# Two transformer layers on one core: quantised probabilities clipped in SBUF and turned by a transposing DMA instead of TensorE, with a new table for the order planner

## What is computed

```
def _fq(x, delta, zp, n_bits):
    xi = _round_ste(x / delta) + zp
    xq = jnp.clip(xi, 0.0, 2.0 ** n_bits - 1.0)
    return (xq - zp) * delta
...
sim = jnp.einsum('bhid,bhjd->bhij', _fq(q, dq, 128.0, 8), _fq(k, dk, 128.0, 8)) * SCALE
attn = jax.nn.softmax(sim, axis=-1)
out = jnp.einsum('bhij,bhjd->bhid', _fq(attn, dw, 0.0, 8), _fq(v, dv, 128.0, 8))
```

## Time and profile before

| | |
|---|---|
| three runs | 3339.07, 3340.45, 3344.31 us, median 3340.45 |
| span of the profiled execution | 3338.1 us (the page gives only its span) |
| the two parts in it | transformer to about 2740 us, experts the rest, 598 us |
| busy over the span | PE 2950.0 us, DVE 2154.6, ACT 1961.0, POOL 1582.2 |

### The profile page before, as it was taken

How to read it: one execution, slowest core, us unless ns; L and a number is a source line. 1 busy time by engine, 2 the same in 40 slices (tenths; PEclk the granted TensorE clock), 3 DMA queues, 4 the chain that set the end, 5 groups by cost and what they waited for, 6 DMA issues and landing times. The chain is left out here.

```text
span 3338.1 us, 59016 instructions
## 1 busy us (share of the span) xinstructions
PE 2950.0 (88%) x19138; PEld 1701.6 (51%) x19138; DVE 2154.6 (65%) x4580; ACT 1961.0 (59%) x4178; POOL 1582.2 (47%) x2774
## 2 busy tenths in 40 slices
PE   6888998999998998989999889988988859999992
PEld 3445443544454354435443544454435229999991
DVE  4887796888678777967896788778556511111115
ACT  3666667576758676676767576757354404444442
POOL 4665472575367355726663575456434321111115
PEclk9999899999999999999999999998988879999996
DMA  3003221422142214313230412141433239999995
GB/s 95 17 23 67 60 65 29 89 61 54 32 86 60 56 37 88 77 29 72 64 69 26 89 45 57 32 86 36 107 77 83 50 76 326 325 327 325 327 323 172
DMA packets 296120, 344.06 MB, mean 103 GB/s; under 512 B 33550, under 2 KB 273294, under 8 KB 295616
## 3 DMA queue, kind: packets, MB, share of 16 engines
q1 hardware_dynamic: 287664, 323.35, 36.0%
q0 software_dynamic: 6480, 17.58, 1.5%
q10 hardware_dynamic: 1728, 0.01, 0.0%
HBM read 291.50 MB, written 51.23 MB: 103 GB/s over the span
## 5 line engine op out<-in xcount | busy, mean ns | idle before, releaser
L1437 ACT ACTIVATE probs<-ps,nbias,sc 128x512 f32<-128x512 f32 x1024 | 790.9, 779 | 284.2 <-DVE nbias L1301 222.6
L1100 POOL TENSOR_SCALAR pq<-probs,rstep 128x512 f16<-128x512 f32 x1024 | 712.0, 695 | 229.3 <-PE ps L1580 144.3
L1318 DVE TENSOR_REDUCE m<-ps 128x1 f32<-128x512 f32 (+3 forms) x1024 | 559.3, 582 | 257.2 <-PE ps L1603 126.8
L1298 DVE TENSOR_REDUCE nmax<-ps 128x2 f32<-128x1024 f32 x512 | 620.5, 1212 | 89.0 <-PE ps L1572 88.5
L1310 DVE TENSOR_SCALAR big<-ps 128x1024 bf16<-128x1024 f16 x512 | 348.0, 680 | 61.5 <-PE ps L1580 59.9
L1603 PE MATMUL ps<-kst,qst 96*128 96x512 bf16 (+3 forms) x1024 | 325.0, 353 | 65.1 <-issue 44.8
L1914 ACT ACTIVATE hT<-moe_ps,e_b 128x128 f32<-128x128 f32 x568 | 208.0, 367 | 281.2 <-PE moe_ps L1868 242.4
L1625 PE MATMUL ps<-qst,kst 108*128 108x512 bf16 (+3 forms) x1024 | 304.0, 352 | 63.0 <-ACT qst L1445 28.3
L1580 PE MATMUL ps<-id,pq 128*128 128x128 f16 x4096 | 320.4, 222 | 44.4 <-DVE big L1310 36.1
L1456 ACT ACTIVATE big<-ps 128x512 f32<-128x512 f32 (+3 forms) x640 | 275.0, 479 | 137.4 <-PE ps L1628 87.6
L1580 PEld LDWEIGHTS ps<-id,pq 128*128 128x128 f16 x4096 | 253.0, 99 | 191.3 <-issue 129.5
(11 more groups left out here) (220 smaller groups left out, 4625.0 us busy)
## 6 DMA issues: line engine op xcount, KB each, us to landing
e_w<-in_L_xattn_e_w_dram SPq DMA_DIRECT2D x142, 1024.0 KB, 7.6
wring<-in_L_xattn_ff_w_dram SPq DMA_DIRECT2D x96, 256.0 KB, 2.9
parts<-parts_sb SPq DMA_DIRECT2D x64, 384.0 KB, 2.4
kst<-parts SPq DMA_DIRECT2D x192, 128.0 KB, 4.4
qst<-parts SPq DMA_DIRECT2D x192, 128.0 KB, 4.7
moe_in<-rows_in SPq DMA_DIRECT2D x71, 140.0 KB, 2.6
xn<-in_ctx_dram SPq DMA_DIRECT2D x16, 512.0 KB, 3.9
got<-rows_out SPq DMA_DIRECT2D x16, 512.0 KB, 6.2
```

Of the source, the lines that this page charges most:

```text
L1100: nc.gpsimd.tensor_scalar(pq[:, u % 2, h, :], probs[:, u % 2, h, :], rstep[:, u % 2, h:h + 1], HALF_ROUND, ALU.mult, ALU.add).then_inc(SIG ...
L1298: nc.vector.tensor_reduce(nmax[:, n % 2, :], ps[:, a:a + 2, :], AX.X, ALU.max, negate=True).then_inc(SIG["M"], 1)
L1318: nc.vector.tensor_reduce(m32[:, g % 2, t, h:h + 1], bank(("A", B, s, n))[:, 0:width], AX.X, ALU.max, negate=True).then_inc(SIG["am"], 1)
L1437: nc.scalar.activation(probs[:, u % 2, h, :], ps[:, BANKS[("S", B, s, u)][h], :], ACT.Exp, bias=nbias[:, u % 2, h:h + 1], scale=sc[:, s:s ...
```

## The change

Four things change in the code.

1. The transposes leave PE. `T`, the PSUM bank view `PT` and the identity `id16` are gone. A new step `dt` on SP issues one `dma_start_transpose` per unit: 128 x 1024 fp16 (256 KB) from SBUF to SBUF, eight 128x128 blocks turned into `probs_t`. `AV` waits for the transfers' semaphores.
2. The clip `ev` stays on DVE, but now reads and writes the same fp16 buffer in SBUF, before the turn. `v_int` and `probs_t` become fp16.
3. The quantised units get four buffers: two in `pq` and two in `rT`, a buffer of the router that is free until the last quantised stage has ended. The small product `rstep` moves from POOL to DVE as a step of its own, `RS`.
4. The planner gets a table of durations in ns (`TIMES`: time on the engine, and time until the result can be used) in place of `TAKES`, `TAIL` and `LANDS`, hops per pair of engines, and `URGENT`, a table of some 150 rows that adds a fixed offset to the urgency of each kind of step by stage and position. Stand-in `W` steps go in at the same threshold.

```diff
-ON = {"PE": "rT rL rP W S T AV A MT B AV2 xT cT k q v y g w z",
-      "DVE": "rl rm ri rp M nb R ev am n1 n3 st dy dz ki qi vi dV dw",
+ON = {"PE": "rT rL rP W S AV A MT B AV2 xT cT k q v y g w z",
+      "DVE": "rl rm ri rp M nb R RS ev am n1 n3 st dy dz ki qi vi dV dw",
...
-      "SP": "LR LX LC psk psq pkk pkq ST"}
+      "SP": "LR LX LC psk psq pkk pkq ST dt"}
...
+TIMES = {
...
+    "do": (569, 687), "dr": (493, 597), "dt": (1500, 3700), "dv": (569, 683), "dw": (666, 750), "dy": (598, 680),
...
+    ("E", 0): (-738, -734, -32912, 172664), ("E", 1): (3001, 365, 107856, -30247), ("E2", 3): (70187, 128776, 13, 17957),
...
+TURNING = 4
...
+            step("RS", B, s, u, ("R", B, s, u))
             for h in range(2):
-                step("Q", B, s, 2 * u + h, ("R", B, s, u), 2 * u + h and ("Q", B, s, 2 * u + h - 1), u >= 2 and ("T", B, s, u - 2))
-            step("T", B, s, u, ("Q", B, s, 2 * u + 1), u >= 1 and ("ev", B, s, u - 1), u == 0 and tail("E2", PAIRED - 1))
+                step("Q", B, s, 2 * u + h, ("RS", B, s, u), 2 * u + h and ("Q", B, s, 2 * u + h - 1), u >= TURNING and ("dt", B, s, u - TURNING))
...
-            step("ev", B, s, u, ("T", B, s, u), u and ("ev", B, s, u - 1), free or None)
+            step("ev", B, s, u, ("Q", B, s, 2 * u + 1), u and ("ev", B, s, u - 1))
+            step("dt", B, s, u, ("ev", B, s, u), u and ("dt", B, s, u - 1), free or None)
...
+    rank = {e: to_end[e] + urgency(*e) for e in steps}
...
-        t, _, e = min([c for c in able if c[1] == engine and c[0] <= first + AHEAD], key=lambda c: (-to_end[c[2]], c[0], number[c[2]]))
+        t, _, e = min([c for c in able if c[1] == engine and c[0] <= first + AHEAD], key=lambda c: (-rank[c[2]], c[0], number[c[2]]))
...
+                if kind == "dt":
+                    g, t, p, i = n // 8, n // 2 % NT, n % 2, NO[e]
+                    after(sp, "ev", B, s, n)
+                    if n % 8 == 0:
+                        half_free(sp, g % 2, e)
+                    sp.dma_start_transpose(probs_t[:, g % 2, 2 * p:2 * p + 2, :, t * P:(t + 1) * P].rearrange("p h j i -> p (h j) i"),
+                                           quantised_unit(i % TURNING).rearrange("p h n -> p (h n)")).then_inc(s_turned[i % TURNING], 16)
...
-                        nc.gpsimd.tensor_tensor(rstep[:, u % 2, :], rinv[:, u % 2, :],
-                                                inv_step[:, 4 * s + 3:4 * s + 4].broadcast_to([P, 2]), ALU.mult).then_inc(s_steps, 1)
-                        pool.wait_ge(s_steps, i + 1)
-                        after_ordinal(pool, "T", i - 2)
-                    nc.gpsimd.tensor_scalar(pq[:, u % 2, h, :], probs[:, u % 2, h, :], rstep[:, u % 2, h:h + 1],
+                        after(pool, "RS", B, s, u)
+                        if i >= TURNING:
+                            unit_turned(pool, i - TURNING)
+                    nc.gpsimd.tensor_scalar(quantised_unit(i % TURNING)[:, h, :], probs[:, u % 2, h, :], rstep[:, u % 2, h:h + 1],
...
                 if kind == "ev":
-                    after(dve, "T", B, s, n)
...
-                    nc.vector.tensor_scalar(probs_t[:, g % 2, 2 * p:2 * p + 2, :, t * P:(t + 1) * P], PT,
-                                            -HALF_ROUND, WMAX, ALU.add, ALU.min).then_inc(SIG["ev"], 1)
+                    after(dve, "Q", B, s, 2 * n + 1)
+                    unit = quantised_unit(NO[e] % TURNING).rearrange("p h n -> p (h n)")
+                    nc.vector.tensor_scalar(unit, unit, -HALF_ROUND, WMAX, ALU.add, ALU.min).then_inc(SIG["ev"], 1)
...
                 if kind == "AV":
...
-                        after(pe, "ev", B, s, 8 * g + 7)
+                        last_turned = NO[("dt", B, s, 8 * g + 7)]
+                        for i in range(last_turned - TURNING + 1, last_turned + 1):
+                            unit_turned(pe, i)
```

More of the change, by code:

```diff
@@ L495, in hop @@
     here, there = ENGINE[e[0]], ENGINE[f[0]]
-    return HOP[there] if here != there else -TAIL[here]
+    if here == there == "SP" and e[0] != "dt":
+        return 100
+    if here == there:
+        return 37 if (e[0], f[0]) in OWN_RESULT else takes(*e) - lasts(*e)
+    return 60 if here == "SP" else 300 if there == "SP" else HOPS[here, there]
 def program_order():
     steps = program_steps()
+    for kind, B, s, n in steps:
+        COUNT[kind, s] = max(COUNT.get((kind, s), 0), n + 1)
     number = {e: n for n, e in enumerate(steps)}
@@ L570, in program_order @@
             order.append(extra)
-            free["PE"] += TAKES["W"]
+            free["PE"] += takes(*extra)
         kind, B, s, n = e
@@ L584, in program_order @@
         free[engine] = t + takes(*e)
-        ended[e] = free[engine] + (LANDS[kind] if kind in LANDS else TAIL[engine])
+        ended[e] = t + lasts(*e)
         order.append(e)
```

130 lines of the change are left out of this document (59 added, 71 removed), and 64 rows, old and new, of tables (MEANS, TAKES, TIMES, URGENT).

## The result

The changed kernel takes 3358.36 us in the median of 5 runs (3348.7 to 3360.86), against 3340.45 (3337.74 to 3347.64, 5 runs) of the kernel before beside it. The ratio from the single runs of both is 1.0042, with an interval from 1.0025 to 1.0058: slower by 0.4% (the two medians alone give 1.0054). The forecast was 3166 us and faster, so both the size and the sign were wrong.

A forecast was written before the change was run, and what follows sets the result against it. PE was taken to bound the quantised stretches, DVE close behind. The middle between PE's -206 and DVE's -141 us, about -174, took 3338.1 to 3164, or 3166 us as run median; 8-in-10 range 3065 to 3310.

The forecast's parts named there:

- PE's relief: Transposes leaving PE in the quantised units: 320.4 us busy and 44.4 us idle ahead of them saved, before added stand-ins.
- DVE's sums: DVE in the quantised units: old clip -348, new clip +213, `RS` +79, waits for POOL +79, together +23 us.
- The waits for POOL: DVE's new clip and `RS` each wait 77 ns per unit for POOL in SBUF, 79 us in all.
- The stand-ins: PE runs 574 more stand-in matmuls at 0.276 us each, costing 158 us.
- PE's own sum: PE's busy time in the transformer part falls by about 160 us: transposes -320.4, stand-ins +158.
- PE's sum of -206 us: By PE alone, time saved: -320.4 - 44.4 + 158 us, with all other PE idle time staying.
- The pace of 2.58 us: DVE as next limit in quantised units: 2.48 us per unit at 96% busy, allowing -141 us over 512 units.
- The transfer, taken at zero: The 256 KB transposing transfer per unit costs nothing, POOL's slack hiding nearly all lateness; at most 128 us.
- The rival in which the transfer bounds the units: Chance 0.07: 1024 packets at 67 ns make each unit's transfer 4.3 us, slower by up to 737 us.
- The order itself: Offsets and durations decide where PE's remaining 264 us of idle go; some tens of us either way, taken as zero.
- DVE over 90% in quantised stretches: Sign for the forecast: DVE over 90% busy there, with PE under 90% but for stand-ins.
- The sign for "wrong" that I named: Prediction wrong if POOL or PE wait over 50 us for transfers, clip reaches 680 ns, or SP's queue delays `dt`.

The follow-up runs named there:

- t_one: The kernel before in its own order, each unit's eight transposes replaced by one 128x512 bf16 matmul, probabilities not turned: 3318.84 us against 3325.73, ratio 0.9970.
- clip_small: The changed kernel with the clip on DVE working on 2 of 1024 columns, order kept: 3316.76 us, ratio 0.9926 to the kernel before.
- turn_plain: The changed kernel with a plain copy of the same 256 KB in place of the transposing transfer: 3294.73 us, ratio 0.9856 to the kernel before.
- order_no_urgent: The kernel before in every operation, ordered by the new planner and durations with all urgency offsets zero: 3378.45 us, ratio 1.0116 to the kernel before.
- w_none: The changed kernel without the stand-in matmuls after the first 40, their waits kept: 3374.74 us, ratio 1.0134 to the kernel before.

## Why the prediction was wrong

The main step that failed is that PE's relief was counted as time, one for one: the same relief by itself was worth 10 us (t_one). Beside it, the relief was mis-sized (92 us instead of 162), and the transfer and the order were put at nothing.

**DVE's sums held.** DVE: forecast +23 us, measured +21.2. The clip: 416 ns forecast, 422 and 424 in the median. The waits for POOL: two times 77 ns per unit forecast; the mean lies above the median by 70 ns for the clip (493 to 423) and 75 for `RS` (232 to 157), and `nb` got 42 ns longer (306 to 348), which I had left out: 187 ns for 154. `nb`'s 18 us more were made up for by 20 us less elsewhere on DVE, which is luck. The stand-ins: 158 us forecast, 365.6 - 222.2 = 143.4 measured.

**PE's own sum did not hold.** `T` is gone with its 320.4, so -177 by these two groups against a forecast -162; on the page, -89.9. A group's busy time counts also the time in which other matmuls are in flight. In the trace of before only 216.1 of the 320.4 us have nothing but transposes in flight, where I took 320.4 and held 282 for the lower price from one set. Time with only transposes or stand-ins in flight fell from 416.6 to 324.6 us, -92.0, and everything else rose by 2.1.

**The step that failed most is the one from sums to time**, in two places.

*PE's sum of -206 us was counted as time*, with the assumption that "all other idle time of PE stays". It did not stay. t_one took the same kind of work away alone and got 10 us for 82 to 114; PE's idle time took the rest, half of it at `S` waiting for `E`. The earlier trace rows show PE at 78.7 of 80 us busy, and I read it as the bound. That stretch holds no stand-ins, and still stages of its kind gained 1 us of 95 in t_one. The 9 us that they gained in the changed kernel need more than PE's relief, then; four buffers for two and the order are the candidates, and no run parts them. The share could not show that `S` depends on a bank that `E` must free. That wait stood in the chain of waits of the kernel before, with 135.0 us, and I did not read it.

*The pace of 2.58 us* took DVE as the next bound at 96%, a share that one window of 40 us had reached, and applied one pace to all units. Over the steady state DVE stays at 80% (989.97 of 1240 us in the changed kernel), as before (980.07), but this mixes two kinds of stage. In the faster kind it is at 89 to 91%, with 77.28 / 31 = 2.49 us of DVE per unit, the 2.48 of the forecast; these stages became longer, from 83 to 86 us. The measured pace in the stages is 86 / 31 = 2.77 us, against 83 / 31 = 2.68 and 95 / 31 = 3.06 before. Only the slow one of the two kinds of stage gained. In clip_small DVE lost 135.5 us of busy time and the kernel 39 us, and the faster kind went from 86 to 81 or 82 us: DVE is on the way, not full. That a late `nb`, `RS` or clip is paid in `E` or `Q` of its unit whatever the share of DVE is my reading, and not shown by a run.

**The transfer, taken at zero**, costs 62 us more than a plain copy in its place (turn_plain). I had three bounds against it: the buffers come round in 10.3 us, the way is 5.1 to 6.9, and a landing stays under 5 us (3.3 measured). All held in the median, and the transfer still cost. The issue was not the 370 ns of a plain one but 1233. SP's queue also stood for the clip for 505 us, with whatever came behind it:

```profile
SPq L1071 <- DVE pq L1392: 305.5, 166, 10.3
SPq L1071 <- DVE rT L1392: 200.0, 131, 7.7
```

But this stand is longer still in turn_plain (640 us), so it is not what the 62 us are. The DMA share of the transformer part rose from 0.26 to 0.54, nearly three tenths where one or two were forecast. The rival in which the transfer bounds the units (4.3 us each) did not come. It had the packets right, 1024 for (828336 - 287664) / 512 = 1056, and their price wrong. The queue's share rose from 36.0 to 59.0%, which is 24 us of one engine per unit: 23 ns a packet for 67, or 1.5 us per unit on 16 engines. What failed is the step that held the transfer to be hidden behind POOL's slack.

**"The order itself", taken at zero**, was the largest single term: 5.1% between offsets and no offsets. The kernel before has no offsets, and it was 1.2% faster with its own plan than with the new numbers (order_no_urgent). A plan is part of a kernel, and the sign of a change in it can't be read off sums of busy time.

**DVE over 90% in quantised stretches**, one of the signs that I named, came in every second stage only, at 89 to 91%. The changed kernel in the window of the earlier trace rows, which is of the other kind:

```profile
560.00:640.00 80.00, 71.52 (x316) 33.38 (x308) 67.40 (x155) 65.09 (x146) 47.09 (x65) 1.00 0.64 134
```

DVE is at 84%, ACT at 81, PE at 89, without a stand-in in this window, and none is full. The sign for "wrong" that I named did come: POOL waits for the transfers for 73.6 us and PE for 28.4, more than 50.

## What to carry to other kernels

Before counting an engine's relief as time, read its longest waits: if what it waits for is the release of a buffer by another engine, the relief can turn into more of that wait, as it did here. A cheap way to know is to thin the operation in the kernel as it stands (t_one) before building the change around it.

In a planned kernel, compare operations under one plan and plans under one set of operations. Offsets found by search fit one program, gain or lose 2 to 5% here, and can hide that the operations underneath got slower. Here the untried course is a search of the same kind for the kernel before: without offsets it starts 4.6% ahead (1.0116 against 1.0579 on the same numbers).

Before counting a group's busy time as an engine's relief, find out how much of it is shared with other instructions of that engine: a third of the transposes' was (104 of 320 us).

Read a pace by kind of stage. Here a mean DVE share of 80% hid stages at 91%, and these are the ones that became longer.

Thin the same operation in both kernels: what it gives in the new one is its price, and not what the change added. And a long wait on a queue is not a price either: SP stood for the clip for 505 us, and for 640 us in the run that was 62 us faster.

## What the runs showed of the hardware

- A transposing transfer of 128x1024 fp16 (256 KB) holds SP's queue for 1233 ns, against 464 to 470 for a plain copy of the same bytes in turn_plain, and adds 467 thousand packets over 512 units, some 912 for each. In all a unit's transfer is 1056 packets. It lands 3.3 us after its issue in the median, 2.7 at the least and 7.7 at the most; the plain copy takes 2.7, 2.2 and 8.4.
- The Trainium skill (VectorE: DVE Perf Modes, section The three transpose paths) gives 1309 ns for one 128x128 block by DMA. Eight blocks one after another would be 10.5 us, an estimate from that page; the runs show 3.3 us to landing for all eight, so blocks overlap or are moved together.
- VectorE and GpSimd lengthen each other in SBUF: a 128x2 `nb` is 348 ns in the mean beside full-size `Q` and clip, 300 with the clip small, 262 with `Q` small; single ones stand for up to 1133 ns. In the other direction a `Q` is 725 ns beside the full clip and 695 beside the small one. This agrees with the rule that the forecast named from the Trainium skill (SBUF — State Buffer, section Who interferes with whom). What it costs in time isn't parted from the operations' own length by these runs.
- The granted clock falls with TensorE's activity taken away: 0.943 in the mean with stand-ins and 0.862 without (w_none), and the kernel was then slower by 0.9 points though TensorE was busy for 192 us less. Most of that was lost in the first 500 us, where the clock of the first two quantised stages was 0.57 and 0.62 for 0.98 and 1.00.
